# Graph layer and routed feed-forward on one core: the first quarters' work placed on other engines and PSUM banks

## What is computed

```python
deg = maximum((adj != 0).sum(-1), 1)
a_norm = rsqrt(deg) * (adj + I) * rsqrt(deg)
x = x + relu((a_norm @ layernorm(x) + layernorm(x)) @ W + b)      # deg here is a column: both factors are the row's
f = layernorm(x)
idx = argmax(f @ gate_w.T)                                         # one of 8 experts for each row, weight 1
h = silu(f @ w1[idx].T) * (f @ w3[idx].T)
x = x + h @ w2[idx].T + gelu(f @ sw1.T) @ sw2.T                    # routed expert, and the shared one
```

## Time and profile before

| | us |
|---|---|
| median of 3 runs (lowest, highest) | 506.79 (506.73, 507.08) |
| the profiled execution | 508.63 |
| its span, first to last instruction | 507.1 |
| PE busy in the span | 456.3 (90%) |
| POOL busy | 326.4 (64%) |
| DVE busy | 271.2 (53%) |
| ACT busy | 198.7 (39%) |

### The profile page before, as it was taken

One profiled execution on the slowest core, in us unless ns is written; L12 is line 12 of the kernel. 1 busy time (PEld: TensorE's weight loads), 2 busy tenths in 40 slices (PEclk: granted clock), 3 DMA queues, 4 the chain that ended last, 5 costly groups with the idle time before them and its releaser, 6 DMA issues.

```text
span 507.1 us, 8982 instructions
## 1 busy us (share of the span) xinstructions
PE 456.3 (90%) x2652; PEld 391.2 (77%) x2653; DVE 271.2 (53%) x552; ACT 198.7 (39%) x435; POOL 326.4 (64%) x305
## 2 busy tenths in 40 slices
PE   5899977999899999889696999699989999999992
PEld 5788756898789878789585888588878888888871
DVE  4998799926694479779053333223343343343330
ACT  3555812563546454845242232123322232232230
POOL 3788867377867795577337484847575757888111
PEclk9899989999999999999888999889999999999996
DMA  7554250502260161793448978787868788365100
GB/s 252 189 180 165 78 161 6 178 2 88 78 208 2 42 209 42 249 343 137 136 125 285 319 242 285 226 273 239 298 226 281 236 268 262 49 76 74 11 1 0
DMA packets 40876, 82.61 MB, mean 163 GB/s; under 512 B 4880, under 2 KB 16528, under 8 KB 38800
## 3 DMA queue, kind: packets, MB, share of 16 engines
q1 hardware_dynamic: 25792, 45.11, 29.0%
q0 software_dynamic: 7536, 29.39, 18.8%
q10 hardware_dynamic: 7520, 7.77, 4.8%
HBM read 74.74 MB, written 8.41 MB: 164 GB/s over the span
## 4 chain that ended last, share of the span: by engine, by line
PE 44%; POOL 12%; DVE 11%; DMA 10%; issue 5%; ACT 3%; ACTq 1%; POOLq 0%; DVEq 0%
PE bank L1224 16%; PE bank L1143 7%; POOL ering L422 6%; PE bank L1251 6%; DMA eraw<-in_experts 5%; PE bank L1163 5%; DVE count L739 4%; DMA ering<-in_experts 4%; POOL a_lo L375 3%; DVE rows L715 3%; PE bank L1252 3%; PE bank L1165 2%; PE bank L1237 2%; POOL gel_lo L391 1%; PE bank L1057 1%
## 5 line engine op out<-in xcount | busy, mean ns | idle before, releaser
L422 POOL TENSOR_TENSOR ering<-eraw,ering 128x512 fp32r<-128x512 f32 x84 | 105.8, 1289 | 69.5 <-DMA ering<-in_experts 36.4
L1224 PE MATMUL bank<-ering,xsT_hi 128*128 x368 | 124.1, 408 | 9.3 <-POOL ering L422 9.3
L375 POOL TENSOR_TENSOR a_lo<-araw,a_hi 128x512 fp32r<-128x512 f32 x64 | 92.5, 1463 | 32.1 <-ACT a_hi L511 31.9
L1057 PE MATMUL bank<-zz,a_hi 128*128 128x512 f32 (+1 forms) x256 | 94.3, 408 | 7.1 <-POOL a_lo L375 7.0
L1224 PEld LDWEIGHTS bank<-ering,xsT_hi 128*128 128x128 f32 x368 | 71.0, 193 | 26.5 <-issue 10.1
L977 DVE SCALAR_TENSOR_TENSOR hid<-bank,xs,sil 128x512 f32<-128x512 f32 x46 | 34.5, 751 | 106.1 <-ACT sil L635 106.1
L1224 PE MATMUL bank<-ering,xsT_lo 128*128 x184 | 74.3, 404 | 0.0
L1059 PE MATMUL bank<-zz,a_lo 128*128 128x256 f32 (+1 forms) x256 | 72.7, 284 | 0.0
L635 ACT ACTIVATE sil<-bank 128x512 f32<-128x512 f32 x46 | 27.5, 598 | 112.9 <-PE bank L1224 112.9
L1251 PE MATMUL bank<-ering,hidT_hi 128*128 x184 | 67.8, 408 | 1.2 <-DVE hidT_lo L985 1.2
L391 POOL TENSOR_TENSOR gel_lo<-gel,gel_hi 128x256 fp32r<-128x256 f32 x58 | 43.8, 757 | 33.6 <-ACT gel_hi L569 33.2
(11 more groups left out here) (152 smaller groups left out, 809.9 us busy)
## 6 DMA issues: line engine op xcount, KB each, us to landing
eraw<-in_experts SPq DMA_DIRECT2D x96, 256.0 KB, 3.7
araw<-in_adj_t SPq DMA_DIRECT2D x32, 512.0 KB, 4.5
ering<-in_experts POOLq DMA_DIRECT2D x8, 1536.0 KB, 8.8
ering<-in_experts POOLq DMA_DIRECT2D x8, 1024.0 KB, 7.1
ering<-in_experts POOLq DMA_DIRECT2D x8, 512.0 KB, 5.5
xs<-sorted_x ACTq DMA_DIRECT2D x23, 129.0 KB, 3.5
resid<-in_x SPq DMA_DIRECT2D x4, 512.0 KB, 9.0
sw_raw<-in_sw_t ACTq DMA_DIRECT2D x2, 1024.0 KB, 6.3
```

The lines of the kernel that those rows point to most:

```text
L375: pool.tensor_tensor(a_lo[:, u % AR, :], araw[:, u // CJ, u % CJ, :], a_hi[:, u % AR, :].bitcast(F32), ALU.subtract).then_inc(adj_lo_ok, 1)
L422: pool.tensor_tensor(ering[:, slot, 1, c * ECW:(c + 1) * ECW], eraw[:, c % ER, :], ering[:, slot, 0, c * ECW:(c + 1) * ECW].bitcast(F32), ...
L1057: pe.matmul(acc(it)[:, :], a_hi[:, s, it * P:(it + 1) * P], zt, start=first, stop=False)
L1224: ins = pe.matmul(bank[2 * w + h][:, :], a[:, k, :], ering[:, bass.ds(slot, 1), part, at:at + BANK].rearrange("p a n -> p (a n)"), start=n ...
```

## The change

Eight edits, all ahead of the experts. (1) The first load of x is split: the first tile comes by itself, is normalized by itself, and its transposes precede the statistics of the other three. (2) The rows of all later norms are made by ACT (`scaled_rows`, with a scale and a `shift` from DVE's new `scales`); DVE's `normalize` stays as `first_rows` for the first 4 tiles. (3) DVE adds b to z straight from PSUM after `z_low`; ACT's copy and POOL's add go. b is loaded later. (4) The shared weights are loaded at tiles 3 and 5 instead of 6 and 9, and split in 8 pieces beside tiles 8 to 15. (5) The sums of quarter 1 lie in banks 4 to 7, and what lay there for quarter 0's transposes, logits and shared blocks goes to banks 0 to 3. (6) `sum_halves` and the first step of `finish_gnn` work in place in PSUM. The banks are free for the next sums (`agg_free`) at the end of `finish_gnn` instead of after `sum_halves`. (7) DVE's order after a quarter is degree, one count, sums, finish, variances, counts; the variances no longer stand after four counts. `choose` comes after them. (8) The steps: `EARLY_RANKS_AT` 3 to 6, `STD_AT` 6 to 4, the norm of quarters 0 to 2 starts at tile 9 instead of 12, tanh moves behind 8 blocks instead of 4.

```diff
@@ steps
-    EARLY_RANKS_AT, STD_AT, THIRD_RANKS_AT, XF_AT, GATE_AT, RANKS_AT = 3, 6, 7, 8, 11, 14
+    EARLY_RANKS_AT, STD_AT, THIRD_RANKS_AT, XF_AT, GATE_AT, RANKS_AT = 6, 4, 7, 8, 11, 14
@@ banks
+        def acc(q, it):
+            return bank[(4 if q == 1 else 0) + it]
+        def degree_bank(q):
+            return bank[1 if q == 1 else 5]
+        def up_bank(m):
+            return bank[(0 if m < 2 * NI else 4) + m % 2]
@@ SP
-            rows_of_x(0)
+            sp.dma_start(resid[:, 0, :], x_in[0:P, :]).then_inc(x_first, 16)
+            sp.dma_start(resid[:, 1:QT, :], x_in[P:QT * P, :].rearrange("(t p) d -> p t d", p=P)
+                         ).then_inc(x_loaded[0], 16)
@@ POOL, first_lows
-                    pool.wait_ge(z_copied, t + 1)
-                    pool.tensor_tensor(norm[:, t, :], norm[:, t, :], bias[:], ALU.add).then_inc(bias_added, 1)
@@ ACT
+            def scaled_rows(k, t):
+                act.wait_ge(scale_ready, k)
+                act.activation(norm[:, t, :], resid[:, t, :], ACT.Identity, bias=shift[:, t % QT:t % QT + 1],
+                               scale=rstd[:, t % QT:t % QT + 1]).then_inc(ln_ready, 1)
...
-                act.activation(norm[:, t, :], bank[6 + t % 2][:, 0:D], ACT.Copy).then_inc(z_copied, 1)
+                if QT <= t + 2 < NT:
+                    scaled_rows((t + 2) // QT, t + 2)
...
+                elif t >= PIECES_AT:
+                    act.wait_ge(shared_loaded, 32)
+                    act.activation(shared_piece(t - PIECES_AT, sw1_hi, sw2_r[:, :, 0, :]),
+                                   shared_piece(t - PIECES_AT, sw1_raw, sw2_raw), ACT.Copy).then_inc(sw_hi_ok, 1)
...
             shared_blocks(LAST, STD_AT)
             stds(2 * NQ - 1)
+            for t in range((NQ - 1) * QT, NT):
+                scaled_rows(2 * NQ - 1, t)
             tanh_of_z(NQ - 2)
@@ DVE
+            def scales(k):
+                dve.wait_ge(std_ready, k + 2)
+                dve.wait_ge(ln_ready, k * QT)
+                chained(dve.reciprocal(rstd[:], std[:]))
+                settle()
+                dve.scalar_tensor_tensor(shift[:], mv[:, :, 0], -1.0, rstd[:], ALU.mult, ALU.mult
+                                         ).then_inc(scale_ready, 1)
...
+                dve.tensor_tensor(norm[:, t, :], bank[6 + t % 2][:, 0:D], bias[:], ALU.add).then_inc(bias_added, 1)
...
+                if t >= PIECES_AT:
+                    i = t - PIECES_AT
+                    dve.wait_ge(sw_hi_ok, i + 1)
+                    dve.tensor_tensor(shared_piece(i, sw1_lo, sw2_r[:, :, 1, :]), shared_piece(i, sw1_raw, sw2_raw),
...
-                    dve.tensor_tensor(agg[:, it, :], acc(it)[:, D:2 * D], agg[:, it, :], ALU.add
-                                      ).then_inc(agg_free, 1)
+                    chained(dve.tensor_tensor(low_sum(q, it), low_sum(q, it), agg[:, it, :], ALU.add))
...
+            inverse_degree(0)
+            count_chunks(1, 0, 1)
             sum_halves(0)
-            inverse_degree(0)
             finish_gnn(0)
+            second_variances(0)
+            count_chunks(1, 1, 2)
@@ PE
+                    if first and q == 1 and it == 1:
+                        pe.wait_ge(dinv_ok, 1)
+                    if first and q >= 2:
+                        pe.wait_ge(agg_free, (q - 1) * QT + it + 1)
```

More of the change, by code:

```diff
@@ L109, in gnn_moe @@
     std = place("std", [P, QT], F32)
+    shift = place("shift", [P, QT], F32)
     deg = place("deg", [P, QT], F32)
@@ L698, in statistics, with aggregates @@
                     chained(dve.bn_stats(stats[:, i, :], resid[:, tiles_of[i], :]))
-            def aggregates():
+            def aggregates(first=0, last=QT):
                 settle()
-                for i in range(QT):
+                for i in range(first, last):
                     dve.bn_aggr(mv[:, i, :], stats[:, i, :]).then_inc(var_ready, 1)
@@ L804, in finish_gnn, with second_variances @@
                 for it, t in enumerate(group(q)):
[L805 to L807 removed]
+                    dve.scalar_tensor_tensor(resid[:, t, :], low_sum(q, it), 0.0, resid[:, t, :],
+                                             ALU.max, ALU.add).then_inc(agg_free, 1)
+            def second_variances(q):
+                dve.wait_ge(agg_free, (q + 1) * QT)
+                dve.wait_ge(scale_ready, NQ + q - 1)
+                variances(group(q))
             def xfT_lows(q):
@@ L904, in _ @@
                     add_shared(2 * (q - 1) + 1)
-            dve.wait_ge(ln_ready, NT + (NQ - 1) * QT)
-            variances(group(NQ - 1))
             choose(NQ - 2)
-            normalize(2 * NQ - 1, group(NQ - 1))
+            scales(2 * NQ - 1)
             place_rows(NQ - 2)
```

193 lines of the change are left out of this document (102 added, 91 removed).

## The result

The changed kernel took **511.7 us** (median of four runs, 509.5 to 512.5) against 506.9 us before: a ratio of **1.0086**, 95% interval 1.0055 to 1.0118. A second set of four runs gave 1.0118 (1.006 to 1.0176). It is slower, by 4.8 us in the first set and by 6.7 in the second. The prediction was 500.1 us, 494.0 to 505.0: a miss of 11.6 us and of the sign.

The account below looks back on a forecast made before the run. PE was taken as the bound nearly everywhere, DVE in quarter 1 and quarter 0's tiles 0 to 11. Terms -0.5 - 7.5 - 1.3 + 2.6 = -6.7 took the 507.1 us span to 500.4, median 500.1; range 494.0 to 505.0.

Parts of the forecast that it names:

- Quarter 1: First product to end of sums: 26.7 us instead of 34.2, a late chunk costing 1.2; -7.5 us.
- The start: Split first load: tile 0's transposes 0.8 us sooner, the second ones 1.4 us later; taken as +1.3 us.
- up to 1 us: At the start: b, asked for at about 10.5 us and needed at 13.5, could add this if late.
- The rest of quarter 0: After the start: waits -3.9, DVE bound in four tiles +2.0, tile 4's row +0.9, POOL's lag -0.8 us.
- the 3.9 us of waits go: Quarter 0: PE's three waits for norm rows vanish, -3.9 us, except about 0.9 at tile 4.
- The pieces: Quarter 0: eight split pieces on DVE, 0.57 to 0.84 us each, together 5.65 us.
- Quarters 2 and 3: Row waits go, -1.7 us; the choice of experts comes later, +0.2 each; -1.3 us in all.
- That wait goes: PE's wait for norm rows vanishes since ACT writes them: 0.85 us in quarter 1, 1.7 in quarters 2 and 3.
- The last shared blocks: Square roots moved ahead: block 4's gelu late, +2.3, uncovered transposes up to +1.0; taken as +2.6 us.
- All of it arrives at the end.: Experts start behind routing and last block, which shift as a whole, so the summed -6.7 us reaches the end.
- (D): Quarter 0: DVE's adds of b cost 1.0 us each, +9.9 us, 510.0 us in all; chance 0.04.
- (C): Quarters 1 to 3: ACT's rows come late and PE still waits, 503.1 to 503.2 us; chance 0.18 shared with another rival.

Follow-up runs that it names:

- run 7: Changed kernel with start, last square roots and sums of quarters 2 and 3 undone, plus weight splits put back in quarter 1: 510.1 us, ratio 1.0064.
- Run 9: On top of run 8, quarter 0's statistics and aggregates one tile earlier, scales ahead of the count: 505.2 us, ratio 0.9975.
- run 4: Changed kernel with the start as before (x in one transfer, b asked for at the start, four rows together): 509.1 us, ratio 1.0028.
- run 3: Changed kernel with the sums of quarters 2 and 3 written to SBUF again: 513.6 us, ratio 1.0123.
- runs 1 and 2: Changed kernel, 1: last square roots back behind block 5, 508.8 us; 2: only ACT's loop behind the square roots written out, 513.2 us.
- run 8: Changed kernel with start, last square roots, quarters 2-3 sums undone; choice ahead of finish in quarter 2, last rows by DVE: 503.1 us, ratio 0.9913.
- Run 6: Kernel before, with 56 extra PE transposes of the identity ahead of block 3 of the last shared blocks: 511.4 us, ratio 1.0092.
- runs 5 and 8: 5: changed kernel with start, last square roots and sums of quarters 2 and 3 undone, 507.4 us; 8: two more edits on top, 503.1 us.

## Why the prediction was wrong, point by point

The aim was right and its size nearly so; four things beside it were wrong. By stage, measured less predicted: start and quarter 0 +3.9, quarter 1 +1.1, quarters 2 and 3 +3.3, last blocks +3.2. These sum to 11.5 us, and the seam and the experts take off 0.4.

- **Quarter 1 (-7.5 predicted, -6.4 measured: -7.3 and -5.6 in the two profiles).** Right, by its steps: counts first, finish in PSUM, rows from ACT, then a chunk as the last bound. The waits for `a_lo` were 1.4 us in two parts in one profile and 2.0 in one in the other, where the forecast had 1.2. The prediction put the two whole splits of the earlier trace rows among the causes, and run 7 bears it out: some 5.5 us hang on them. What was off is that counts took 1.93 us on average beside POOL and not 1.45.
- **The start (+1.3 predicted, +3.2 measured).** Tile 0's transposes came sooner than forecast (6.5 and 7.25 us, not 7.5), and so did the second ones (10.2 and 11.2, not 11.3). The step that failed is b: it was written down as "up to 1 us" and taken at nothing. Its transfer took 5.7 us from issue, and DVE stood 1.8 to 2.3 us for it with the low parts of the next tile behind. Of the 1.4 us that the forecast did charge, DVE's low part of tile 1 shows 0.7 on average (11.8 us against 11.1 with the old start). That PE would stand 3.35 us behind tile 0's transposes, and that the clock could fall to 1.2 GHz there, I had not forecast either; but the profile with the slow clock began quarter 1 sooner than the one without (59.2 and 60.0).
- **The rest of quarter 0 (-1.8 predicted, +0.2 measured).** The term that failed is "the 3.9 us of waits go". With the old start PE still waited 3.3 us for rows, at three tiles as before, and I had charged 0.9 for one tile. The reason is the one that the prediction itself gave two sentences later: DVE is as busy as before. Run 9 shows that the waits are DVE's load under another name. Besides, the longest of them (2.1 us) is followed by a dip of the clock in six of the eight profiles that run 4 speaks of, and quarter 1 begins 0.4 to 2 us later in these; the forecast had no dip there. I booked the wait as won and DVE's load as a separate cost, where they are one thing. Terms that were right: b's add at 0.38 to 0.415 us (measured 0.412), POOL's lag at the end (1.0 us before, none after). The pieces cost 0.6 us by one pair of profiles, not 2.0. Not priced at all was `shift`: 0.60 us on average on four columns, beside POOL. ACT's row took 0.60 us against the 0.38 that I took from a gelu. The gelu's source is in PSUM and the row's in SBUF, but that is little of it: ACT's copy `gel_hi` of the same size, with its source in SBUF, took 0.42. What the row has besides is a scale and a shift from columns. That mattered little here and 0.6 us in the last blocks.
- **Quarters 2 and 3 (-1.3 predicted, +2.0 measured).** Two steps failed. "That wait goes" held for the rows, but `a_lo` took the place: 1.3 to 1.4 us a quarter instead of 0.6. The forecast asked what is late next in quarter 1, and not in these. And of the finish it said that it is shorter, and priced only what stands behind it on DVE. It missed who waits for its end: PE's first `shared_down` of a pair of half quarters, 1.5 us, since the banks hold the sums until the last step. The choice was forecast right: it is ready 9.95 us behind the end of quarter 2's sums, where the forecast had 9.9, and PE would be there at about that time, as run 3 shows. PE does not wait for it.
- **The last shared blocks (+2.6 predicted, +5.8 measured).** The chain on ACT was right: 2.5 us longer (6.94 against 4.42), where I had 2.35. The place of it was not. The up to 1.0 us for uncovered transposes was taken at 0.3; runs 1 and 2 put the place at 2.5 us, with the slower clock behind a wait of 5.1 us in it where there was one. The rows on ACT, taken off in run 8, are worth 2.5 us. The finish's 1.5 us wait stands there too; run 3 removed it, and the stage took 27.9 us, as in the changed kernel (28.0).
- **"All of it arrives at the end."** Run 6: of 6.1 us, 4.4, with an interval (2.8 to 6.5) that just takes in all of it.
- **The rivals.** None had this outcome for its mechanism. (D) ended on the right side, at 510.0, for a wrong reason: b's adds cost what I had said. (C), rows that come late, was half right in quarter 0. What none of them held is that several parts add a wait each, and of the last blocks only the size was doubted, not the sign.
- **The range** took in the unknown prices of operations, and no missed wait. Two of the missed waits (banks free at the finish's end, b late for DVE's first add) could have been found in the code by asking for each `wait_ge` whose semaphore is now raised later who stands behind it. That a difference of 0.2% can be told was too hopeful as well: intervals of these comparisons reach 0.2 to 0.6% to either side.

By the Trainium skill's "SBUF — State Buffer", section "SBUF: two separate sides", a DVE operation with two SBUF inputs and a GpSimd one that reads SBUF hold a shared port for their whole length in turn. The rows agree in kind: `a_lo` takes 1.29 us with DVE idle (at 109.53) and 1.69 on average beside counts, and a count 1.2 alone and 1.93 beside POOL. The prediction called the four operations of 3.63 us in the earlier trace rows the finish's first step; they are its second, and the first took 2.65. In the prediction I used the rule for what the PSUM forms win on DVE. It also says what happens to POOL when DVE's counts stand closer together, and the waits for `a_lo` are what took the place of those for rows.

## What to carry to other kernels

- A wait for an engine that is busy without a gap isn't won by moving the operation that is waited for; it comes back at the next thing that the engine owes. Book the engine's load or the wait, not both.
- When a semaphore is raised later than before, go through everyone who waits for it, also far from the place that is edited. When the undoing makes an operation slower, it can bring a wait of its own as long as the one that goes, so a time that doesn't change doesn't show that the wait cost nothing.
- A long wait is cheapest where PE has other work in line for it (the transposes at block 8), and it can cost more than its length, when the clock falls behind it.

## What the runs showed of the hardware that I had not expected

- A DVE operation on 128x4 values took 0.93, 0.69 and 1.04 us beside POOL's `a_lo`, and each time it ended within 0.03 us of it (29.57 and 29.54, 41.21 and 41.19, 71.80 and 71.79 us). With POOL idle it took 0.16 us.
- An ACT operation on 128x256 values with a scale and a shift from columns took 0.60 us (0.52 in a row of four). A copy of that size took 0.42 us with its source in SBUF and 0.38 with its source in PSUM. So most of the difference is not the source; whether it is the columns or the function, no run here tells.
- Waits of 2 us sometimes brought the granted clock down and sometimes not, with the same code: 40 to 50 us of runs 5 and 8 had 1.00 and 0.85, and quarter 1 began 1.9 us later in the latter. The gap of 3.35 us at the start was followed by 0.53 in one profile of the changed kernel and by 1.00 in the other. Quarters 0 and 1 of the same kernel differed by 2.5 us between two profiles of the changed kernel, and the expert stage by 5.1 us (244.7 and 249.8). What sets the expert stage's length (from PE's arrival at the third expert to the end of the step there it lay between 13.5 and 19.2 us, where a step without a wait takes 9.5) stayed open; run 6 shows only that a later front didn't change it.
